# A Perceiver block on one Trainium2 core: cross-attention in another order of work, with the row maxima subtracted by 32-row products

## The reference

```python
x = x + _L0_xattn_ref(_layernorm(x, axis=-1), ctx_1024, Wq1, Wk1, Wk2, Wv1, Wv2, Wo, bo)
x = x + _L0_attn_ref(_layernorm(x, axis=-1), ...)
x = x + _L0_ffn_ref(_layernorm(x, axis=-1), ...)

def _L0_xattn_ref(x1, x2, Wq1, Wk1, Wv1, Wk2, Wv2, Wo, bo):   # 8 heads of 64
    q1, k1, v1 = x1 @ Wq1, x1 @ Wk1, x1 @ Wv1
    k2, v2 = x2 @ Wk2, x2 @ Wv2
    k, v = concatenate([k1, k2]), concatenate([v1, v2])       # 256 + 4096 keys
    attn = softmax(einsum("bihd,bjhd->bhij", q1, k) * 64 ** -0.5)
    return einsum("bhij,bjhd->bihd", attn, v) @ Wo + bo
```

## Time and profile before

| | |
|---|---|
| median of the runs | 1687.1 us |
| the profiled execution, its own time | 1682.5 us |
| its span, first to last instruction | 1680.8 us |
| PE busy | 1475.6 us (88%) |
| DVE busy | 1128.8 us (67%) |
| ACT busy | 711.3 us (42%) |
| POOL busy | 448.6 us (27%) |
| cross-attention on PE | 15.2 to 1179 us |
| mean granted TensorE clock | 0.963 of full speed |

### The profile page before, as it was taken

How to read it: one execution, slowest core, us unless ns; L and a number is a source line. 1 busy time by engine, 2 the same in 40 slices (tenths; PEclk the granted TensorE clock), 3 DMA queues, 4 the chain that set the end, 5 groups by cost and what they waited for, 6 DMA issues and landing times. The chain is left out here.

```text
span 1680.8 us, 29549 instructions
## 1 busy us (share of the span) xinstructions
PE 1475.6 (88%) x11988; PEld 1130.3 (67%) x11988; DVE 1128.8 (67%) x1287; ACT 711.3 (42%) x954; POOL 448.6 (27%) x270
## 2 busy tenths in 40 slices
PE   5999999999999999999999999999497787826996
PEld 4777776776776677677667777777264444526996
DVE  4587578557657855865876586486586899654663
ACT  3444344434434433343444344344336333223773
POOL 4300024000002400000230010000122999533885
PEclk9999999999999999999999999999799999967998
DMA  5000021000002100000210000000203900092333
GB/s 172 13 11 11 1 86 48 1 14 11 11 14 73 48 1 14 13 9 14 86 35 1 14 20 1 2 1 2 83 1 137 276 1 0 1 324 93 58 63 59
DMA packets 62371, 76.50 MB, mean 46 GB/s; under 512 B 6368, under 2 KB 47968, under 8 KB 61840
## 3 DMA queue, kind: packets, MB, share of 16 engines
q1 hardware_dynamic: 57152, 68.51, 13.3%
q0 software_dynamic: 5088, 6.11, 2.5%
HBM read 58.39 MB, written 17.25 MB: 45 GB/s over the span
## 5 line engine op out<-in xcount | busy, mean ns | idle before, releaser
L496 DVE TENSOR_REDUCE xa_maxes<-psum 128x2 f32<-128x1024 f32 (+1 forms) x288 | 332.5, 1161 | 268.9 <-PE psum L677 268.9
L422 ACT ACTIVATE xa_probs<-psum 128x1024 f32<-128x1024 f32 x272 | 269.1, 1026 | 325.4 <-PE psum L710 312.5
L517 DVE TENSOR_TENSOR xa_prob_sum<-xa_prob_sum,xa_probs 128x1024 f32<-128x1024 f32 x240 | 308.8, 1287 | 11.2 <-ACT xa_probs L422 10.4
L722 PE MATMUL psum<-xa_probs,xa_vals 128*64 128x256 f32 x2176 | 263.1, 385 | 2.2 <-DVE xa_heads_T L531 1.6
L722 PEld LDWEIGHTS psum<-xa_probs,xa_vals 128*64 128x64 f32 x2176 | 146.5, 136 | 92.7 <-issue 23.6
L347 POOL TENSOR_TENSOR xa_w_lo<-xa_stage,xa_w_hi 128x768 fp32r<-128x768 f32 x16 | 31.9, 1994 | 615.4 <-ACT xa_w_hi L382 615.4
L609 PE MATMUL psum<-xa_wv_hi,xa_ctx_hi 128*128 128x256 f32 x512 | 148.3, 290 | 21.2 <-DVE xa_maxes L496 18.4
L704 PE MATMUL psum<-xa_q_hi,xa_k_hi 64*128 64x256 f32 x1088 | 157.2, 285 | 0.6 <-issue 0.6
L708 PE MATMUL psum<-xa_q_hi,xa_k_lo 64*128 64x256 f32 x1088 | 155.1, 281 | 0.0
L710 PE MATMUL psum<-xa_neg_max,xa_ones 64*128 64x256 f32 x1088 | 154.7, 280 | 0.0
L706 PE MATMUL psum<-xa_q_lo,xa_k_hi 64*128 64x256 f32 x1088 | 154.5, 280 | 0.0
(11 more groups left out here) (319 smaller groups left out, 3013.1 us busy)
## 6 DMA issues: line engine op xcount, KB each, us to landing
xa_ctx_in<-in_ctxT_dram SPq DMA_DIRECT2D x32, 512.0 KB, 3.7
ex_slots<-mx_blank_tile SPq DMA_DIRECT2D x2, 4372.5 KB, 37.1
xa_stage<-in_L_xattn_Wk_dram SPq DMA_DIRECT2D x32, 128.0 KB, 2.4
xa_stage<-in_L_xattn_Wv_dram SPq DMA_DIRECT2D x16, 256.0 KB, 2.9
ex_raw<-in_L_ffn_w_gate_dram SPq DMA_DIRECT2D x8, 512.0 KB, 10.5
ex_raw<-in_L_ffn_w_up_dram SPq DMA_DIRECT2D x8, 512.0 KB, 10.9
ex_raw<-in_L_ffn_w_down_dram SPq DMA_DIRECT2D x8, 512.0 KB, 12.1
ex_xt<-ex_slots SPq DMA_DIRECT2D x15, 265.0 KB, 2.8
```

Source lines behind the costliest of these rows:

```text
L422: nc.scalar.activation(probs[:, n % RING, :], S[:, 2 * (n % 2):2 * (n % 2) + 2, :].rearrange("p h q -> p (h q)"), ACT.Exp, scale=HD ** -0. ...
L496: dve.tensor_reduce(maxes[:, qt, :, g:g + 1], max_banks(v, g, qt)[:, :, 0:group_keys(g)[1]], AX_X, ALU.max).then_inc(max_reduced, 1)
L517: dve.tensor_tensor(prob_sum[:, :], prob_sum[:, :], probs[:, n % RING, :], ALU.add).then_inc(summed, 1)
L722: i = pe.matmul(O[half[h], 0:N1], vals[:, 2 * j + t, lanes:lanes + HD], probs[:, n % RING, (2 * h + t) * N1:(2 * h + t + 1) * N1], start=( ...
```

## The change

**Row maxima.** `subtract_maxima` runs once a step, ahead of the scores: one product of 32 rows and 512 columns for each tile and head, four in a step of two tiles, each in its own quarter of the rows and in its own bank of the four in S; they open the accumulation, and the scores add to them. For that the four rows 0, 32, 64 and 96 of `neg_max` hold the maxima (two small reductions by DVE in place of one).

**Order.** Steps with value products place the first tile's `weigh` between the key and the value products. In step 8 the `weigh` of tiles 14 and 15 stand between the `score_for_max`, that of tile 16 behind them. The queries of unit u+2 are projected at the end of step 8, ahead of `turn_maxima`. The weights are split in two parts: those of queries and of the latents' keys (512 columns) at step 6, the rest (256) at step 8. The context chunks are split four steps later. The latents of the next batch are turned by PE at step 0 of unit 4b+2 (`turn_own`) and split from there by ACT and DVE, so `xl_T` goes. At the start only the first batch's latents (256 KB) are loaded ahead of the first weights; the others are normalized while the first unit is prepared.

```diff
-            for t in range(TT):                      # PE, start
-                pe.wait_ge(norm.done, norm.tiles_done(0, t + 1))
...
+            def turn_own(b):
+                pe.wait_ge(norm.done if b == 0 else norm_rest.done, ...)
+                if b > 0:
+                    pe.wait_ge(q_split, b * PAIRS)
+                for t in range(QT):
+                    for c in range(DC):
+                        i = pe.transpose(KQ[...], src[:, c * P:(c + 1) * P], ident[:, :])
+                i.then_inc(own_turned, 1)
...
+            def subtract_maxima(u, tiles):
+                pe.wait_ge(neg_max_ready, u + 1)
+                n = u * HG + tiles[-1]
+                if n >= 2:
+                    pe.wait_ge(exp_done, n - 1)
+                for k, (j, h) in enumerate(itertools.product(tiles, range(2))):
+                    rows = slice(k * P // 4, (k + 1) * P // 4)
+                    pe.matmul(S[:, 2 * ((u * HG + j) % 2) + h, :], ones[rows, :],
+                              neg_max[rows, :].unsqueeze(1).broadcast_to([P // 4, 2, N1]),
+                              start=True, stop=False)
...
             def score(u, j):
-                if n >= 2:
-                    pe.wait_ge(exp_done, n - 1)
-                if j == 0:
-                    pe.wait_ge(neg_max_ready, u + 1)
...
-                        pe.matmul(out[h], k[h], q[h], start=True, stop=False)
+                        pe.matmul(out[h], k[h], q[h], start=False, stop=False)
...
-                        i = pe.matmul(out[h], ones[half[h], :], neg_max[half[h], :], start=False, stop=True)
...
             for u, d in steps():
...
-                    project_queries(v)
                     project_keys(v, 0, v * NG * QT, values)
+                    if own_due(u, d) is not None:
+                        turn_own(own_due(u, d))
                 if following and d >= 1:
                     score_for_max(v, d - 1, 1, values)
+                subtract_maxima(u, step_tiles(d))
...
+                if following and d < STEPS - 1:
+                    score_for_max(v, d, 0, values)
...
+                    project_keys(v, d + 1, maxima, values)
+                    if d == 0 and u > 0:
+                        sum_probs(u - 1)
+                    for j in weighed[0:1]:
+                        weigh(u, j)
+                    for c, j in v_due(u, d):
+                        project_values(c, j, maxima)
+                    for j in weighed[1:2]:
+                        weigh(u, j)
+                elif following:
+                    weigh(u, weighed[0])
+                    score_for_max(v, d, 0, values)
+                    weigh(u, weighed[1])
+                    score_for_max(v, d, 1, values)
+                    weigh(u, HG - 1)
+                    for c, j in v_due(u, d):
+                        project_values(c, j, maxima)
+                    if u + 2 < U:
+                        project_queries(u + 2)
+                    turn_maxima(v, values)
...
-            at = (u % PAIRS - 2) * STEPS + d - 3          # chunk_due
+            at = (u % PAIRS - 2) * STEPS + d - 7
...
-            sp.dma_start(X1[:, :, :], ...).then_inc(x_loaded, 16)      # SP, start: then bo, wo, load_pair(0)
+            sp.dma_start(X1[:, 0:QT, :], ...).then_inc(x_loaded, 16)
             load_pair(0)
+            load_chunk(0, 0)
+            load_values(0)
+            load_chunk(0, 1)
+            sp.dma_start(X1[:, QT:TT, :], ...).then_inc(rest_loaded, 16)
+            sp.dma_start(bo_sb, ...).then_inc(rest_loaded, 16)
+            for c in range(2, CHUNKS):
+                load_chunk(0, c)
+            sp.dma_start(wo_sb[:, :, :], ...).then_inc(rest_loaded, 16)
...
             for g in range(NG):                           # DVE, first unit
                 split_keys(0, g)
+                if g == 1:
+                    dve.wait_ge(rest_loaded, 48)
+                    norm_rest.prepare(dve, 0, X1[:, QT:TT, :])
```

More of the change, by code:

```diff
@@ L120, in normalize, with apply, done_prepared @@
                                  ALU.mult).then_inc(done, 2)
-        dve.wait_ge(done, at + 2 * n + 6)
-        for t in range(n):
-            dve.tensor_scalar(out[:, t, :], x[:, t, :], self.agg[:, t, 0:1], self.rstd[:, t:t + 1],
-                              ALU.subtract, ALU.mult).then_inc(done, 1)
+    def apply(self, dve, calls, x, out, t):
+        self.done_prepared(dve, calls)
+        dve.tensor_scalar(out[:, t, :], x[:, t, :], self.agg[:, t, 0:1], self.rstd[:, t:t + 1],
+                          ALU.subtract, ALU.mult).then_inc(self.done, 1)
+    def done_prepared(self, dve, calls):
+        dve.wait_ge(self.done, calls * self.per_call + 2 * self.n + self.STEPS)
+    def normalize(self, dve, calls, x, out):
+        self.prepare(dve, calls, x)
+        for t in range(self.n):
+            self.apply(dve, calls, x, out, t)
     def root(self, act, calls):
@@ L189, in cross_attention @@
         x_loaded = sem("xa_x_loaded")
[L190 removed]
+        rest_loaded = sem("xa_rest_loaded")
+        norm = Norm(sb, sem, "xa_norm", QT)
+        norm_rest = Norm(sb, sem, "xa_norm_rest", TT - QT)
         setup = sem("xa_setup")
@@ L262, in k_pieces, with own_due @@
             return [(at, 1, 0), (0, 1, 1)]
+        def own_due(u, d):
+            return u // PAIRS + 1 if d == 0 and u % PAIRS == 2 and u + 2 < U else None
         def v_due(u, d):
@@ L371, in _ @@
                     split_chunk(u // PAIRS + 1, c)
+                if d == 6 and u + 2 < U:
+                    split_query_weights(u + 2)
                 if d == STEPS - 1 and u + 2 < U:
@@ L423, in exponentials @@
                     "p h q -> p (h q)"), ACT.Exp, scale=HD ** -0.5).then_inc(exp_done, 1)
+            norm.root(act, 0)
+            split_query_weights(0)
             split_weights(0)
-            norm.root(act, 0)
+            store_own_hi(0)
+            split_chunk(0, 0)
             split_values_weights(0)
-            for c in range(AHEAD):
-                split_chunk(0, c)
-            act.wait_ge(xl_transposed, TT)
             store_q_hi(0)
+            split_chunk(0, 1)
             for g in range(NG):
@@ L546, in _ @@
                         reduce_max(0, g - 1, qt)
+                if 2 <= g < 5:
+                    for t in (2 * g - 4, 2 * g - 3):
+                        norm_rest.apply(dve, 0, X1[:, QT:TT, :], xl_next, t)
             for qt in range(QT):
@@ L554, in _ @@
                 if d == 0:
+                    if v < U:
+                        split_keys(v, 0)
+                        if own_due(u, d) is not None:
+                            split_own(own_due(u, d))
                     if u > 0:
@@ L638, in project_keys @@
                     pe.wait_ge(q_split, v + 1)
+                    if v % PAIRS == 3 and v + 1 < U:
+                        pe.wait_ge(own_split, b + 2)
                 elif g >= 2:
@@ L707, in score @@
                     for h in range(2):
-                        pe.matmul(out[h], k[2 + h], q[h], start=False, stop=False)
-                    for h in range(2):
-                        i = pe.matmul(out[h], ones[half[h], :], neg_max[half[h], :], start=False, stop=True)
+                        i = pe.matmul(out[h], k[2 + h], q[h], start=False, stop=(t == 1))
                 i.then_inc(scores_ready, 1)
@@ L745, in project_output @@
                 i.then_inc(out_projected, 1)
+            pe.wait_ge(ident_ready, 1)
+            turn_own(0)
+            pe.wait_ge(setup, 3)
             project_queries(0)
-            for g in range(NG):
+            for g in range(NG - 1):
                 project_keys(0, g, 0, 0)
@@ L754, in _ @@
                         score_for_max(0, g - 1, qt, 0)
-            for qt in range(QT):
-                score_for_max(0, NG - 1, qt, 0)
+            project_keys(0, NG - 1, 0, 0)
+            for qt, j in enumerate(group_tiles(NG - 1)):
+                score_for_max(0, NG - 2, qt, 0)
+                project_values(0, j, 0)
+            score_for_max(0, NG - 1, 0, 0)
+            project_queries(1)
+            score_for_max(0, NG - 1, 1, 0)
             values = HG
```

150 lines of the change are left out of this document (83 added, 67 removed).

## The result

The changed kernel takes 1676.7 us (median, 1674.5 to 1678.6) against 1687.1 (1684.5 to 1692.7): ratio 0.9937, 95% interval 0.9921 to 0.9953. It is faster by 10.4 us, or 0.6%, which the interval keeps clear of no change; forecast were 22 us.

The account below looks back on a forecast made before the run. The prediction took PE's list, its changes of shape and its waits to bound the kernel. Its terms, +20.6 + 28 - 65 - 6 = -22, taken off the median 1687.1 gave 1665 us; range of 8 in 10: 1638 to 1695.

Parts of the forecast that it names:

- The maxima, +20.6: Row maxima in the cross-attention: 64.7 us of products out, 33.8 in, 51.5 for 264 changes of shape; a loss of 20.6.
- Rival 1: Row maxima: the four 32-row products don't run side by side; 1699 us two by two, 1766 one after another; chance 0.12.
- rival 2: Row maxima: changes between 64 and 32 rows cost nothing, giving 1615 us; chance 0.08.
- Other changes of shape, +28: Cross-attention: 164 more changes, nearly all visits to `weigh` between key and value products and in step 8, mean 0.17 us.
- Waits, -65: PE's waits in the cross-attention steps and at changes of batch go, 65 us in sum.
- changes of batch and even steps 8: PE's waits at three changes of batch go, 22 us, and those of the first `score_for_max` in even step 8, 4.5.
- step 8 of odd units: Seven such steps: `weigh` covers each reduction that `score_for_max` and the values wait for, 14 us gained.
- even step 1: Step 1 of seven even units: the values' wait for DVE mostly goes, 9 us gained.
- the term of -16: Odd units, steps 2 to 7: `weigh` fills the values' wait for bank M behind the keys, 16 us gained.
- The start, -6: Up to the first scores: earlier queries and context keys, PE going on at 30.5 us; 6 us gained, bounds 0 and 12.
- Rival 3: Cross-attention: waits move instead of going, DVE's list being nearly as long as PE's in even steps; 1687 us, chance 0.22.

Follow-up runs that it names:

- experiment 1: Changed kernel with the row maxima as before (four pairs of 64-row products a tile, inside the scores), new order kept: 1656.7 us, ratio 0.9825.
- experiment 3: Changed kernel with the group of maxima in its place but of 64 rows, as two pairs of 512 columns one behind the other: 1658.7 us, ratio 0.9832.
- experiment 6: Changed kernel with both `weigh` of a step behind the value products again in steps 2 to 7 of odd units: 1673.0 us, ratio 0.9933.
- experiment 5: Changed kernel with `sum_probs` behind the value products again in step 0 of the even units: 1672.6 us, ratio 0.9925.
- experiment 9: Changed kernel with the edits of experiment 1, experiment 5 and experiment 7, and ScalarE's part of a context chunk directly behind the exponentials: 1641.4 us, ratio 0.9737.
- experiment 2: Kernel before with only the row maxima changed to the 32-row group ahead of the scores, old order kept: 1696.3 us, ratio 1.0056.
- experiment 4: Changed kernel with the statistics of the other latents waiting for the latents alone, not for the bias and Wo: 1670.8 us, ratio 0.9906.
- experiment 7: Changed kernel with the edit of experiment 4, and the other batches' statistics one group later, behind the reductions: 1667.2 us, ratio 0.9888.
- experiment 11: Changed kernel with the 32-row group directly behind `weigh`, ahead of `score_for_max`: 1673.1 us, ratio 0.9921.

## What the prediction had right, and which steps failed

Forecast was a gain of 22 us, measured are 10.4. The way and the cost of the maxima were right; the sum of the waits and the start were not.

- **The maxima, +20.6.** Right: 20.0 by the medians of experiment 1. Rival 1 is refuted (four side by side, 0.50 for all), rival 2 too (0.195 for each change of height), and experiment 3 isolates the height. (The time of rival 2 should have read 1613 or 1614, 1665 less 51.5, not 1615.) The estimate worked out from the Trainium skill (TensorE: Matmul & The Clock Gate, Measured speedup vs the span model), 0.31 a group and 10 us more, is not borne out: the four last 0.50 us together, as two 64-row products of 512 columns do. The rule of the Trainium skill (TensorEngine Tiling (Array Packing), Key Properties) that a change of the tiling mode drains the engine agrees with the traces: 0.195 us for a change between 64 and 32 rows, nothing between the two halves.
- **Other changes of shape, +28.** The number of changes was right (421 more between first and last score, of 428 in all), and that is all that the 75.7 for 79.5 of the table shows. Their price has one test, experiment 6: 0.33 for the two around a `weigh`, where I had 0.34.
- **Waits, -65.** This sum failed, by 12 us. The places that I had rows for came near: with the transposes where the forecast had them, the changes of batch and even steps 8 gave 23 of 26.5, step 8 of odd units 14 of 14, and even step 1 gave 11 of 9. Two things were missing. First, even step 0: I listed waits that go and took `sum_probs` for work that is merely elsewhere. It had been the cover of ScalarE's copy, and without it the values' last bank is late: +5.6 us where I had put nothing, seen in experiment 5. I had written myself that a cover gone costs what is late behind it, looked for it in VectorE alone, and never asked it of ScalarE. Second, steps 3 to 6 of units 3, 7 and 11: context chunks that are split four steps later meet VectorE's addition of the sums. That costs 0.24 (9.64 for 9.40) in 12 steps, 3 of the 5 us that the term of -16 lacks (experiment 9); the other 2 are within what the split of the table can tell. The move of `weigh` in steps 2 to 7 paid nothing in the forecast's own terms either (13 us of wait against 42 x 0.34 = 14 of changes of shape), and it is a loss, since the group of maxima by itself would have filled half of that wait (experiments 2 and 6).
- **The start, -6.** Failed: 0 was gained in the profiled execution, the lower of my bounds, and 1 or 2 us if the other runs with this start are counted in. The stop for `rest_loaded` was in the forecast, but too small: Wo landed at 29.1 and not at 25, and PE went on at 33.8 and not 30.5. It gained 1.1 us on the earlier trace rows (33.80 for 34.92) and lost that behind it, by slow products: the mean granted clock up to the first score is 0.91, where it was 0.96 before. Experiments 4 and 7 give what was to be had, 9.6 us between the two first scores and 9.5 between the medians: wait for what is needed, and put the statistics behind the reductions.
- **Rival 3** (the waits move, VectorE's list is long) was nearer than its 0.22: it is right in kind at two places, and its 1687 is 10 us off where the forecast is 12 off; but 53 of the 65 us did go.

Together 15 us too much: 12 in the waits and 6 in the start, less some 3 in the other terms. By the medians the error is 12.

## What to carry to other kernels

Before work is moved away from a place, list what ends while it runs, on every engine, and who wants the buffers: work that gains nothing where it stands may be a cover. A product that saves columns but changes the array's height or width is paid for twice, in and out (0.385 us here, more than the 0.24 of PE time that the low group saves in a step); count the changes as carefully as the columns. And a saving ahead of a wait for a reduction, or a cost ahead of it, goes into that wait: know the slack of each pair "product, reduction, next product in the same bank" first.

## What the runs showed of the hardware that was not expected

- Four 32-row products in the four quarters run fully side by side (0.50 us for x4 of 512 columns), but a change between 64 and 32 rows costs as much as one between 64 and 128: 0.195 us. Between the halves of one height there is none.
- VectorE's addition of two operands in on-chip memory takes 1.22 us alone. Started while GpSimd's subtraction there runs, it ends 1.08 to 1.21 us behind that one's end (182 additions in fourteen traces), and so takes up to 2.5. VectorE's reductions out of PSUM beside the same subtraction keep their 1.21 to 1.23 (28 in the changed kernel).
- A wait can cost more than its length: in experiment 11 PE waits a tenth of a microsecond for a bank, and the keys behind `score_for_max`, of another shape, start another 0.11 late. So it is in 90 of its steps (0.43 for 0.32); in seven others with such a wait it is 0.32 all the same, so this is no rule.
